# Unkept candidates of the second attention as a bfloat16 product with minus twice the identity, cut at zero by the eviction

## What is computed

```python
def _L1_attn_ref(x, Wq, bq, Wk, bk, Wv, bv, Wo, bo, entropy_ema, entropy_threshold):
    B, L, D = x.shape                      # 8 items, 256 positions, 128 features
    H, dh = (N_HEADS, D_HEAD)              # 16 heads of 8
    ...
    attn = jax.nn.softmax(scores, axis=-1)
    sr = MIN_SPARSITY + (1.0 - MIN_SPARSITY) * jax.nn.sigmoid(entropy_ema - entropy_threshold)
    k_keep = jnp.maximum(1, (L * (1.0 - sr)).astype(jnp.int32))
    ...
    keep = rank < k_keep[None, :, None, None]
    w = jnp.where(keep, attn, jnp.float32(0.0))
    w = w / (jnp.sum(w, axis=-1, keepdims=True) + 1e-10)
    out = jnp.einsum('bhqk,bhkd->bhqd', w, v)
    out = out.transpose(0, 2, 1, 3).reshape(B, L, D)
    return out @ Wo.T + bo
```

## Time and profile before

| | |
|---|---|
| three runs | 2082.57, 2087.64, 2089.56 us |
| span of the profiled execution | 2115.3 us |
| PE busy / its weight loads | 1667.9 us (79%) / 1254.0 us (59%) |
| DVE busy | 1496.8 us (71%) |
| ACT busy | 1114.1 us (53%) |
| POOL busy | 877.9 us (42%) |
| mean granted TensorE clock, passes 0 to 6 | 0.85 of full speed |
| same, pass 7 | 0.93 |

### The profile page before, as it was taken

How to read it: one execution, slowest core, us unless ns; L and a number is a source line. 1 busy time by engine, 2 the same in 40 slices (tenths; PEclk the granted TensorE clock), 3 DMA queues, 4 the chain that set the end, 5 groups by cost and what they waited for, 6 DMA issues and landing times.

```text
span 2115.3 us, 40910 instructions
## 1 busy us (share of the span) xinstructions
PE 1667.9 (79%) x13664; PEld 1254.0 (59%) x13664; DVE 1496.8 (71%) x4747; ACT 1114.1 (53%) x3322; POOL 877.9 (42%) x1162
## 2 busy tenths in 40 slices
PE   3888899986287887887779867625777889999978
PEld 2445667764177787787778546512444367777763
DVE  6788766546688998898886732347776587888557
ACT  1444444437888788889732422202453266776620
POOL 3333221033334345344322566465411176776610
PEclk8899999986588888888889978856795899999979
DMA  4111101003000000000001022222101000000000
GB/s 136 47 48 41 33 29 32 17 5 120 16 9 9 16 9 10 16 16 2 1 2 57 27 65 91 99 62 64 52 29 76 14 1 2 1 1 2 2 1 20
DMA packets 67314, 67.72 MB, mean 32 GB/s; under 512 B 9955, under 2 KB 58966, under 8 KB 66566
## 3 DMA queue, kind: packets, MB, share of 16 engines
q1 hardware_dynamic: 58930, 53.09, 7.6%
q0 software_dynamic: 5120, 10.50, 1.8%
q10 hardware_dynamic: 3040, 1.38, 0.2%
HBM read 30.41 MB, written 8.39 MB: 18 GB/s over the span
## 4 chain that ended last, share of the span: by engine, by line
PE 41%; DVE 22%; ACT 17%; issue 11%; ACTq 3%; another core or an unknown queue 3%; POOL 2%; DMA 1%; SPq 1%; DVEq 0%; POOLq 0%
DVE weights L3150 4%; ACT rope_s L4230 3%; ACT rope_c L4230 3%; PE bank L2139 3%; PE bank L1547 3%; PE bank L2099 3%; ACT big L4440 3%; PE bank L1563 3%; PE bank L1740 2%; PE bank L1741 2%; ACTq L4063 2%; PE bank L2126 2%; PE bank L1376 2%; PE bank L1400 2%
## 5 line engine op out<-in xcount | busy, mean ns | idle before, releaser
L2707 DVE TENSOR_REDUCE nmax<-bank 128x4 f32<-128x1024 f32 x144 | 175.9, 1222 | 59.3 <-PE bank L1327 47.7
L887 POOL TENSOR_TENSOR big<-big,rinv 128x512 f32<-128x512 f32 x128 | 131.6, 1049 | 45.8 <-DVE rinv L3762 45.8
L1754 PE MATMUL bank<-V,probsT 128*128 128x9 f32 x1024 | 129.8, 257 | 21.7 <-ACT probsT L4241 21.7
L1754 PEld LDWEIGHTS bank<-V,probsT 128*128 128x128 f32 x1024 | 129.2, 199 | 27.0 <-ACT probsT L4241 25.2
L4045 ACT ACTIVATE feat_o<-bank 128x1024 f32<-128x1024 f32 x72 | 73.7, 1023 | 103.8 <-PE bank L1327 72.7
L1740 PE MATMUL bank<-const,big 128*128 128x128 f32 x512 | 118.5, 318 | 12.2 <-DVE hid L3207 8.9
L4440 ACT ACTIVATE big<-bank,nmax 128x256 f32<-128x256 f32 x256 | 117.6, 477 | 11.1 <-DVE nmax L3756 11.1
L4241 ACT ACTIVATE probsT<-bank 128x512 f32<-128x512 f32 x128 | 75.5, 595 | 91.0 <-PE bank L1741 65.6
L4045 ACT ACTIVATE O<-bank 128x1024 f32<-128x1024 f32 x72 | 73.7, 1023 | 94.1 <-PE bank L1327 68.2
L3756 DVE TENSOR_REDUCE nmax<-bank 128x2 f32<-128x512 f32 x128 | 82.0, 683 | 58.1 <-PE bank L2099 58.1
L1741 PE MATMUL bank<-silu_b,hid 128*128 128x128 f32 x512 | 116.2, 315 | 0.0
(11 more groups left out here) (806 smaller groups left out, 5252.9 us busy)
## 6 DMA issues: line engine op xcount, KB each, us to landing
qT<-parts SPq DMA_DIRECT2D x276, 32.0 KB
big<-V SPq DMA_DIRECT2D x192, 32.0 KB
y_rows<-weights SPq DMA_DIRECT2D x24, 256.0 KB
big<-parts SPq DMA_DIRECT2D x180, 32.0 KB
weights<-in_weights_l_ffn SPq DMA_DIRECT2D x1, 4832.0 KB, 14.8
weights<-in_weights_l_attn SPq DMA_DIRECT2D x1, 3904.0 KB, 12.9
qT<-V SPq DMA_DIRECT2D x96, 32.0 KB
weights<-in_weights_l_ffn SPq DMA_DIRECT2D x1, 2860.0 KB, 11.3
```

What stands on the lines that cost most here:

```text
L887: nc.gpsimd.tensor_tensor(row, row, rinv[:, h % H, :].unsqueeze(2).to_broadcast([P, T, S]), ALU.mult).then_inc(scaled.sem, 1)
L1754: last = mm(pb[1][:, t * S + h * wide:t * S + (h + 1) * wide], probsT[:, h % 2, at:at + P], values_of(b, k)[:, h * wide:(h + 1) * wide], s ...
L2707: V_.tensor_reduce(to, scored.rearrange("p (i a n) -> p i a n", i=HPG, n=n), AX.X, ALU.max, negate=True).then_inc(score_max.sem, 1)
```

## The change

The unkept elements are no longer left in `cands` as float32. `mark` writes them as bfloat16 over the bits of the same group, which nobody reads any more by then (`unkept = at_most`). PE multiplies these by minus twice the identity in bfloat16, so that an unkept element comes out as a number near minus itself, and ACT evicts with Relu in place of Copy, which makes it zero. As the bits of a group now live until PE has turned it, ten groups of them are held in a ring rather than eight (`BIT_GROUPS`). `candidates` waits only for the marking of the group four ahead of it, and `count_kept` waits for the turning of the group ten ahead of it.

```diff
-        halves_of_bits = region[1][:, DOWN_AT:DOWN_AT + ROWS1 * S // 2].bitcast(BF16)
-        at_most = halves_of_bits.rearrange("p (j k) -> p j k", k=S)
+        low_bits = region[1][:, DOWN_AT:DOWN_AT + (GROUPS + 1) * GROUP_WORDS].bitcast(BF16).rearrange("p (g j k) -> p g j k", j=4, k=S)
+        bit_groups = [low_bits[:, g] for g in range(GROUPS + 1)] + [O[:, 0, GROUP_WORDS:2 * GROUP_WORDS].bitcast(BF16).rearrange("p (j k) -> p j k", k=S)]
+        at_most = lambda b, g: bit_groups[(b * GROUPS + g) % BIT_GROUPS]
+        unkept = at_most
...
-        neg_ident = silu_b[:]
+        minus_two = silu_b[:, 0:P // 2].bitcast(BF16)
...
-                    pool.wait_ge(probsT_psum.sem, probsT_psum(ph, used // GROUPS, 2 * (used % GROUPS) + 2))
+                    pool.wait_ge(marked_ready.sem, marked_ready(ph, used // GROUPS, used % GROUPS + 1))
...
-                        last = mm(pb[6 + h % 2][:, at], cands[g % CANDS][:, 2 * (h % 2) + t, keys], neg_ident, start=False, stop=True)
+                        last = mm(pb[6 + h % 2][:, at], unkept(b, g)[:, 2 * (h % 2) + t, keys], minus_two, start=False, stop=True)
...
+                    used = b * GROUPS + j // 4 - BIT_GROUPS
+                    if j % 4 == 0 and used >= 0:
+                        dve.wait_ge(probsT_psum.sem, probsT_psum(ph, used // GROUPS, 2 * (used % GROUPS) + 2))
...
-                    row = cands[g % CANDS][:, j, :]
-                    last = V_.match_replace(row, largest[:, g % 2 * 4 + j, :], row, 0.0)
+                    last = V_.match_replace(unkept(b, g)[:, j, :], largest[:, g % 2 * 4 + j, :], cands[g % CANDS][:, j, :], 0.0)
...
-                nc.scalar.activation(probsT[:, h % 2, :], pb[6 + h % 2][:], ACT.Copy).then_inc(probsT_ready.sem, 1)
+                nc.scalar.activation(probsT[:, h % 2, :], pb[6 + h % 2][:], ACT.Relu).then_inc(probsT_ready.sem, 1)
```

More of the change, by code:

```diff
@@ L57 @@
 CANDS = 4
+BIT_GROUPS = GROUPS + 2
+GROUP_WORDS = 4 * S // 2
 QUICK_STEPS = 3
@@ L1142, in candidates @@
                     used = b * GROUPS + g - CANDS
-                    pool.wait_ge(probsT_psum.sem, probsT_psum(ph, used // GROUPS, 2 * (used % GROUPS) + 2))
+                    pool.wait_ge(marked_ready.sem, marked_ready(ph, used // GROUPS, used % GROUPS + 1))
                 for two in (slice(0, 2), slice(2, 4)):
-                    at_most_g = at_most[:, 4 * g + two.start:4 * g + two.stop, :]
-                    last = nc.gpsimd.tensor_tensor(cands[g % CANDS][:, two, :], group_of(b, g)[:, two, :], at_most_g, ALU.mult)
+                    last = nc.gpsimd.tensor_tensor(cands[g % CANDS][:, two, :], group_of(b, g)[:, two, :], at_most(b, g)[:, two, :], ALU.mult)
                 last.then_inc(cand_ready.sem, 1)
@@ L2993, in bisect @@
                     linkup()
-                link(V_.memset(at_most, 0.0))
-                for early in cands:
+                for early in [at_most(b, g) for g in range(GROUPS)] + cands:
                     link(V_.memset(early, 0.0))
@@ L3149, in count_kept @@
                 for j in range(first, end):
-                    last = V_.tensor_scalar(at_most[:, j, :], row_of(b, j), tried[at][:, 0, j:j + 1], 0.0, ALU.is_le, ALU.add,
+                    used = b * GROUPS + j // 4 - BIT_GROUPS
+                    if j % 4 == 0 and used >= 0:
+                        dve.wait_ge(probsT_psum.sem, probsT_psum(ph, used // GROUPS, 2 * (used % GROUPS) + 2))
+                    last = V_.tensor_scalar(at_most(b, j // 4)[:, j % 4, :], row_of(b, j), tried[at][:, 0, j:j + 1], 0.0, ALU.is_le, ALU.add,
                                             accum_out=tried[at][:, 1, j:j + 1])
@@ L3252, in l1_attn @@
                 dve.wait_ge(pass_done.sem, pass_done(ph, 0, 1))
-                link(V_.tensor_scalar(neg_ident, C("ident"), -1.0, None, ALU.mult))
+                link(V_.tensor_scalar(minus_two, C("ident"), -2.0, None, ALU.mult))
                 l1_intake(1)
```

## The result

The changed kernel takes 2106.51 us (median of 4 runs, 2101.26 to 2113.95), and the kernel before 2085.11 us. The ratio is 1.0098, with a 95% interval of 1.0077 to 1.0118: about 20 us slower, where 23 us faster was forecast.

A forecast was written before the change was run, and what follows sets the result against it. DVE was taken to bound passes 0 to 6 and PE pass 7; -16 + 3 - 10 = -23 us, scaled to -22.7, gave 2087.6 - 22.7 = 2065 us, own range 2056 to 2074, overall range 2049 to 2083.

The forecast's parts named there:

- What bounds the kernel: Second attention: DVE works 456.1 of 512.9 us in passes 0 to 6; in pass 7 the chain lies on PE.
- (c): Passes 0 to 6: PE with less work is throttled, mean clock 0.57; pass 7's gain cancels, 2087 us; chance 0.08.
- (d): Passes 0 to 6: throttled PE at clock 0.56 takes 76.1 us a pass, so slower, 2097 us; chance 0.06.
- The product: PE's bfloat16 product for a float32 one: saves 0.16 us, 0.32 at half rate, or only 0.11 if loading isn't hidden.
- Passes 0 to 6: DVE's waits for ACT's counts, scores and the doubt's sum shrink: -16 us, ends -20.4 and -8.
- The counts' wait: DVE's wait in `second_move` for ACT, passes 0 to 6: 11.5 of 14.7 us go.
- The scores and the doubt: DVE's waits for PE in passes 0 to 6: 4.5 of their 5.7 us go, as PE's queue is shorter.
- the term for POOL: Passes 0 to 6: POOL's moved products hold up DVE, +8 beside `second_move`, -5 at ends of passes, net +3 us.
- POOL's products: POOL's candidates stop waiting for PE and collide with DVE elsewhere: net +3 us, ends +17 and -8.
- Added at nothing: `mark` writing bfloat16, Relu for Copy, and the new waits of `count_kept` and `candidates` cost nothing.
- Pass 7: PE's 64 cheaper products save 11.0 us, or 8.1 at the low end; taken as -10 us.

The follow-up runs named there:

- e3_thin: The kernel before, float32, with the second product of each pair only 32 of its 128 columns wide: 2302.58 us, ratio 1.1026.
- e9_after_wide: The changed kernel with the weighing's products 117 or 126 columns wide in place of 9, same result: 2068.1 us, ratio 0.9915.
- e10_before_wide: The kernel before with the weighing's products 117 or 126 columns wide in place of 9: 2083.21 us, ratio 0.9982.
- e5_relu: The kernel before, second product still float32 and full width, with minus twice the identity and ACT evicting with Relu: 2082.75 us, ratio 1.0001.
- e4_poolwait: The changed kernel, but POOL's candidates wait for PE's turning again, as before the change: 2105.16 us, ratio 1.0079.

## Why the prediction was wrong

**What bounds the kernel** was read rightly: DVE in passes 0 to 6, PE in pass 7. DVE's busy time did not change (456.1 and 456.0 us), and its waits account for the whole of the growth.

**The step that failed is the rate at which PE's work was priced.** The sum took the saving at the clocks of before, 0.85 and 0.93, and gave a falling clock 0.14 together, in (c) and (d), with the words that "the products come in long runs, and PE keeps more than two thirds of each pass busy". Long runs and a busy PE do not hold the clock: with the change PE is busy 88% of the passes and 95% of pass 7 and is granted 0.64 and 0.68. In these runs the clock moved with the widths of the products: thinner ones in float32 brought it to 0.50 (e3_thin), and wider ones in the changed kernel brought it back to 0.84 (e9_after_wide), each without any other edit. The rows for this were in the prediction: the weighing's 9-column instructions take as long as those with 128, so in them PE mostly loads weights.

Rivals (c) and (d) came nearest, with 2087 and 2097 us, for a wrong reason and with a wrong point. They had PE slow down by idling. And they let it cost nothing until PE's work fills a pass, at 0.57; in the traced run 0.64 was enough for 20.9 us of waits, since DVE waits for single late products (the doubt's sum 16.2 us, scores 11.0 us) long before PE's total reaches the pass. They also took 10 us of gain in pass 7 for granted, where the clock fell too and PE's run grew from 45.7 to 51.5 us (1119.97 to 1171.50).

**The product** was mis-sized within its bounds: 0.11 us saved, not 0.16. The forecast chose the end at which the next float32 load is hidden. The float32 product took 0.27 us for 0.22, which fits a load that is not hidden, though no run tried this by itself. The eight products of the earlier trace rows could not show it: there bfloat16 stands behind float32, and what costs is float32 behind bfloat16.

**Passes 0 to 6 with the clock up:** -16 + 3 = -13 was forecast. e9_after_wide against e10_before_wide has 503.3 against 509.0 us, -5.7, and not from the waits that the forecast named. DVE's waits went from 40.2 to 39.5 us in all, where -16 was forecast. The counts' wait fell by 2.8 us (12.9 to 10.1), not by 11.5: a product of head 0 has only 0.22 us to gain at the half rate, not 0.32, and the rest of this miss was not traced. The scores and the doubt had only 0.9 us of waits left to give, and the register reads of `settle_doubt` took 2.1 us more. It is DVE's busy time that fell by 5.3 us (458.6 to 453.3), by the term for POOL: the search steps took 2.7 us more, and DVE's guess, doubt and statistics at the ends of passes (`l1_guess`, `doubt`, `l1_stats`) 8.4 us less. So -5.7 where +3 was forecast.

**POOL's products** in the changed kernel itself: the seven search steps take 34.5 us against 29.8 before, +4.7 where +8 was forecast, and in passes 1 to 4 they take 6.2 to 6.6 us each where 7 was forecast. Guess, doubt and statistics at the ends of passes take 8.4 us against 15.2, -6.8 where -5 was. So the net is -2 and not +3: the mechanism came in both places, and the sizes were off. Here are POOL and DVE in the changed kernel's pass 2, start, us and line, with the idle time before them:

```profile
768.41 4.50 POOL L1149 TENSOR_TENSOR feat_o<-big,weights 128x512 f32<-128x512 f32 x4
...
766.91 0.23 DVE L3104 TENSOR_TENSOR small<-small,routes 128x32 f32<-128x32 f32 x1 [0.91 <-ACTq L4238]
...
769.57 1.16 DVE L3117 TENSOR_TENSOR small<-routes,small 128x32 f32<-128x32 f32 x1
...
772.99 0.19 DVE L3125 TENSOR_TENSOR small<-small 128x32 f32<-128x32 f32 x1
```

Groups 6 and 7 follow each other without the wait for PE, 768.41 to 772.91, right beside the step (766.91 to 773.18), as the prediction had it.

**Added at nothing** held for all edits that were tried: Relu and the factor show no cost (e5_relu), match_replace with a bfloat16 result takes 409 ns for 408, and no comparison waits for PE at L3155, which does not stand among the waits above.

```profile
L3211 DVE MATCH_REPLACE8 weights<-small,hid 128x256 bf16<-128x256 f32 x116 | 46.1, 409 | 0.0
L3155 DVE TENSOR_SCALAR_CACHE_REDUCE weights<-weights,small 128x256 bf16<-128x256 f32 x84 | 34.4, 474 | 0.0
```

These are DVE's groups in the attention of the changed kernel, with the columns of the earlier trace rows; a 0.0 at the end says that nothing was waited for.

**Pass 7:** -10 was forecast. With the clock at 0.92 in both (e10_before_wide and e9_after_wide) it is -7.7 (48.7 to 41.0 us), near 64 x 0.11 = 7.0.

**What stays open:** in the kernels with the ring of bits one of the seven register reads of `settle_doubt` takes about 6 us (5.9 at L3191, "issue" in the waits above), some 2 us longer than the others. Its cause was not tried. Open too is how much of the 20 us POOL's earlier products took at the low clock (e4_poolwait), and which property of PE's work the granted clock follows: the runs show that it moved with the widths of the products, not why.

## What to carry to other kernels

Before making products on TensorE cheaper, look at what will be left between them: a saving at the full rate can be more than lost if the thinner mix runs at the half rate, as here, where 15 us of gain became 20 us of loss. Busy time does not show the risk, since an engine that loads weights counts as busy; compare the widths of the products with their pace. Where the pace is set by loading, extra columns cost little (0.118 us an instruction for 0.109 here), and they turned 20 us of loss into a gain of 18 us, about 4 of which the kernel before gains by the width too.

## What was not expected of the hardware

TensorE's clock fell from 1.00 to 0.50 and stayed there for 26 us in a stretch in which PE was busy without a gap. Cutting 96 of 128 columns from 512 products that kept their pace at the half rate (0.85 us a pair against 0.86) made the kernel 215 us slower, and repeating 9 columns 14 times made the changed one 38 us faster.
